# Value weights times the sums of four batches, a store for each head, loops written out

## The reference

```python
qh = (q_in @ wq + bq).reshape(b, q_len, H, K)          # b 8, q_len 112, H 16, K 128
kh = concat((kv_in @ wk + bk).reshape(b, t, H, K), bias_k)   # t 375, +1
vh = concat((kv_in @ wv + bv).reshape(b, t, H, K), bias_v)
weights = softmax(einsum('bqhk,bthk->bhqt', qh, kh) / sqrt(K))
ctx = einsum('bhqt,bthk->bqhk', weights, vh)
x = x + ctx @ wo + bo
```

## Time and profile before

| | us |
|---|---|
| median of 3 timed runs | 2390.0 (2389.4 to 2391.0) |
| the profiled execution | 2393.2 |
| its span, first to last instruction | 2391.3 |
| PE busy in it | 2313.3 (97%) |
| DVE busy | 1342.9 (56%) |
| ACT busy | 1146.4 (48%) |
| POOL busy | 376.4 (16%) |
| granted TensorE clock, mean | 0.995 of full |

### The profile page before, as it was taken

How to read it: one execution, slowest core, us unless ns; L and a number is a source line. 1 busy time by engine, 2 the same in 40 slices (tenths; PEclk the granted TensorE clock), 3 DMA queues, 4 the chain that set the end, 5 groups by cost and what they waited for, 6 DMA issues and landing times.

```text
span 2391.3 us, 45273 instructions
## 1 busy us (share of the span) xinstructions
PE 2313.3 (97%) x13859; PEld 2103.7 (88%) x13859; DVE 1342.9 (56%) x3154; ACT 1146.4 (48%) x2531; POOL 376.4 (16%) x739
## 2 busy tenths in 40 slices
PE   6899899999999999999999999999999999999999
PEld 5677678888999998999998788999998999998888
DVE  5677774443556555565554514555565555554743
ACT  4677752354445544445453444454444455453421
POOL 4011126430000100100101120001001001002421
PEclk9999989999999999999999999999999999999999
DMA  5322126474455645645635464455545546544110
GB/s 167 123 77 84 61 80 220 176 238 138 162 184 184 192 172 183 206 170 181 225 129 169 174 180 130 167 186 188 202 163 179 206 162 211 193 137 153 58 54 31
DMA packets 232451, 376.32 MB, mean 157 GB/s; under 512 B 57278, under 2 KB 185682, under 8 KB 232258
## 3 DMA queue, kind: packets, MB, share of 16 engines
q1 hardware_dynamic: 232258, 373.87, 47.0%
HBM read 315.77 MB, written 58.05 MB: 156 GB/s over the span
## 4 chain that ended last, share of the span: by engine, by line
PE 90%; DVE 3%; issue 3%; ACT 3%; DMA 0%; ACTq 0%; SPq 0%; DVEq 0%
PE ps_k L1508 10%; PE ps_k L1509 9%; PE ps_k L1510 9%; PE ps_o L1508 9%; PE ps_o L1510 8%; PE ps_o L1509 8%; PE ps_v L1508 6%; PE ps_v L1509 6%; PE ps_v L1510 6%; PE ps_s L1508 4%; PE ps_s L1510 4%; PE ps_s L1509 4%; PE ps_t L1667 3%; PE ps_t L1607 1%; PE ps_o L1619 1%
## 5 line engine op out<-in xcount | busy, mean ns | idle before, releaser
L1508 PE MATMUL ps_k<-cs_hi,w_a_hi 128*128 128x376 f32 x1152 | 391.7, 340 | 7.0 <-DVE k_lo L1284 4.3
L1509 PE MATMUL ps_k<-cs_lo,w_a_hi 128*128 128x376 f32 x1152 | 385.4, 335 | 0.0
L1510 PE MATMUL ps_k<-cs_hi,w_a_lo 128*128 128x376 f32 x1152 | 384.2, 333 | 0.0
L986 ACT ACTIVATE prob<-ps_s,row_columns 112x376 f32<-112x376 f32 x256 | 147.2, 575 | 300.3 <-DVE row_columns L1290 300.3
L767 POOL CAST k_hi<-xk_hi 128x1 fp32r x256 | 47.0, 184 | 1274.4 <-PE ps_s L1510 1274.4
L1508 PEld LDWEIGHTS ps_k<-cs_hi,w_a_hi 128*128 128x128 f32 x1152 | 217.3, 189 | 12.6 <-DVE k_lo L1284 8.8
L1509 PEld LDWEIGHTS ps_k<-cs_lo,w_a_hi 128*128 128x128 f32 x1152 | 217.5, 189 | 0.1
L1510 PEld LDWEIGHTS ps_k<-cs_hi,w_a_lo 128*128 128x128 f32 x1152 | 217.0, 188 | 0.0
L1284 DVE SCALAR_TENSOR_TENSOR k_lo<-ps_k,col_b,k_hi 128x375 fp32r<-128x375 f32 x256 | 155.2, 606 | 99.3 <-ACT k_hi L954 94.7
L954 ACT ACTIVATE k_hi<-ps_k,col_b 128x375 fp32r<-128x375 f32 x256 | 146.3, 572 | 102.2 <-PE ps_k L1510 99.3
L731 POOL TENSOR_TENSOR w_b_lo<-w_raw_b,w_b_hi 128x512 fp32r<-128x512 f32 x88 | 120.0, 1391 | 420.4 <-ACT w_b_hi L817 420.3
(11 more groups left out here) (256 smaller groups left out, 5964.0 us busy)
## 6 DMA issues: line engine op xcount, KB each, us to landing
ckd_hi<-context_by_key_halves SPq DMA_DIRECT2D x64, 768.0 KB, 4.3
ckd_lo<-context_by_key_halves SPq DMA_DIRECT2D x64, 768.0 KB, 5.8
cs_hi<-context_halves SPq DMA_DIRECT2D x64, 752.0 KB, 5.9
cs_lo<-context_halves SPq DMA_DIRECT2D x64, 752.0 KB, 7.3
w_raw_b<-in_blocks_b SPq DMA_DIRECT2D x104, 256.0 KB, 3.9
w_raw_a<-in_blocks_a SPq DMA_DIRECT2D x104, 256.0 KB, 4.6
q<-q_scratch SPq DMA_DIRECT2D x72, 224.0 KB, 5.7
shared<-extra_probability SPq DMA_DIRECT2D x32, 448.0 KB, 4.6
```

Of the source, the lines that this page charges most:

```text
L986: act.activation(prob[buf][0:LQ, 0:KW], ps_s[buf][0:LQ, 0:KW], ACT.Exp, bias=max_neg[0:LQ, buf:buf + 1], accum_out=prob_sum[0:LQ, buf:buf ...
L1508: pe.matmul(out, w_h, m_h, start=first, stop=False)
L1509: pe.matmul(out, w_h, m_l, start=False, stop=False)
L1510: return pe.matmul(out, w_l, m_h, start=False, stop=last)
```

## The change

- **Four batches at once.** Sums are kept for four batches (`sums`, a quad) and a head's product has 448 columns: 12 matmuls a head and quad. The heads of a quad come in steps 0 and 1 of the second batch of the next quad (`quarter == 1`), two a step; all other batches have one sum a step. Between heads there is one bank as before.
- **One `term` buffer** instead of two, with 448 columns. ACT's term of head t waits for DVE's add of head t-1.
- **One store a head**: four stores of 224 KB for each quad in 448-byte pieces, from two buffers `o_head`; `output` of head t waits for the store of head t-2. The SP queue stores heads 0 and 1 right after `load_halves`, heads 2 and 3 after `store_extra`.
- **The extra probabilities** are loaded once a quad, for four batches.
- **All five loops are written out** (`range` in place of `Fori`).
- **First attention**: the scores of tile t+2 are made before the weighted sums of tile t, and two tiles' scores stand in the prologue.
- **The MLP's end**: rows 0 and 1 are scaled before the weight splits, not after.
- Buffers of stages that don't overlap share memory.

```diff
+        self.quads = blocks * QUADS + pair // 2
+        self.quarter = self.b % 4
...
+        sums_hi = sb("sums_hi", [P, DT, 4 * HALF], F32R)
...
+        sums_lo = sb("sums_lo", [P, DT, 4 * HALF], F32R)
...
+        extra_b = extra[:, 0:4 * NT * LQ].rearrange("p (b r t) -> p b t r", b=4, t=NT)
+        term = extra[:, 4 * NT * LQ:5 * NT * LQ].rearrange("p (b r) -> p b r", b=4)
...
+        o_head = [o_all[:, HALF * i:HALF * (i + 1)].rearrange("p (b r) -> p b r", b=4) for i in range(2)]
...
-            with eng.Fori(1, 3) as fg:
+            for fg in range(1, 3):
                 mlp(0, fg, 1, RT * (fg + 1))
             mlp(0, 3, 1, RT * 4, norm=2)
...
-            with eng.Fori(0, 2) as a:
+            for a in range(0, 2):
...
-            with eng.Fori(1, PAIRS - 1) as p:
+            for p in range(1, PAIRS - 1):
...
-            with eng.Fori(1, GROUPS - 1) as group:
+            for group in range(1, GROUPS - 1):
...
-            if place.parity == 0:
+            if place.quarter != 1 or place.head:
                 return (t,)
             return {2: (0, 1), 3: (2, 3)}.get(t, ())
...
-            return (2 * t, 2 * t + 1) if place.parity and not place.head and t < 2 else ()
-
-        def second_late(place, t):
...
+            return (2 * t, 2 * t + 1) if place.quarter == 1 and not place.head and t < 2 else ()
+
+        def quad_before(place):
...
-                def store_pair(place):
-                    sp.wait_ge(z_ev, NT * place.pairs + NT)
+                def store_head(place, t):
+                    sp.wait_ge(z_ev, NT * place.quads + t + 1)
                     sp.sem_inc(sp_waited, 1)
-                    dst = o_scr[ds(place.group, 1), ds(2 * place.pair, 2)].rearrange("g b p f -> p (g b) f")
-                    sp.dma_start(dst, o_all[:, 0:2 * NT * LQ].rearrange("p (b f) -> p b f", b=2)).then_inc(z_out, 16)
+                    b0 = place.b - place.quarter
+                    dst = o_scr[place.group, b0:b0 + 4, :, t * LQ:(t + 1) * LQ].rearrange("b p r -> p b r")
+                    sp.dma_start(dst, o_head[t % 2]).then_inc(z_out[t % 2], 16)
...
-                    if not place.head:
-                        sp.wait_ge(z_term, NT * place.pairs)
-                        sp.sem_inc(sp_waited, 1)
-                    src = pex_scr[ds(place.block, 1), ds(2 * place.pair, 2)].rearrange("o b f -> o (b f)")
-                    sp.dma_start(shared[:, 0:2 * NT * LQ], src.partition_broadcast(P)).then_inc(extra_in, 16)
+                    wait(sp, z_term, NT * place.quads)
+                    sp.sem_inc(sp_waited, 1)
+                    src = pex_scr[ds(place.block, 1), ds(place.b - 3, 4)].rearrange("o b f -> o (b f)")
+                    sp.dma_start(extra[:, 0:4 * NT * LQ], src.partition_broadcast(P)).then_inc(extra_in, 16)
...
+                    for head in heads(place, 0):
+                        store_head(quad_before(place), head)
                     store_extra(place)
-                    if place.parity:
-                        if not place.head:
-                            store_pair(pair_before(place))
+                    for head in heads(place, 1):
+                        store_head(quad_before(place), head)
+                    if place.quarter == 3:
                         load_extra(place)
...
-                    if t >= 2 or not place.head:
-                        act.wait_ge(z_ev, NT * place.pairs + t - 1)
+                        act.wait_ge(extra_in, 16 * place.quads + 16)
+                    wait(act, z_ev, NT * place.quads + t)
                     act.sem_inc(act_waited, 1)
-                    act.activation(term[t % 2], extra_b[:, :, t, :], ACT.Identity,
+                    act.activation(term, extra_b[:, :, t, :], ACT.Identity,
...
-                for r in range(3 if norm is not None else 0):
-                    deviation(norm, r)
+                if norm is not None:
+                    for r in range(3):
+                        deviation(norm, r)
+                    scaled(norm, 0)
+                    scaled(norm, 1)
+                    deviation(norm, 3)
                 split_hi(0, na + 1, range(4), lambda s: (h_mm, HIDDEN * (4 * m + fg) + HIDDEN - 4 + s + 1))
                 if norm is None:
                     split_hi(1, nb + 1, range(4), lambda s: (y_mm, x0 + RT))
-                for r in (3, 4) if norm is not None else ():
-                    deviation(norm, r)
-                    for row in TURNS_LATE[r]:
+                if norm is not None:
+                    deviation(norm, 4)
+                    for row in (2, 3, 4):
                         scaled(norm, row)
-                if norm is not None:
-                    scaled(norm, 3)
-                    scaled(norm, 4)
                     deviation(norm, 5)
                     deviation(norm, 6)
...
-                    dve.wait_ge(z_mm, NT * place.pairs + t + 1)
-                    dve.wait_ge(z_term, NT * place.pairs + t + 1)
-                    if t == 0 and not place.head:
-                        dve.wait_ge(z_out, 16 * place.pairs)
-                    if t == 0 and place.head:
+                    dve.wait_ge(z_mm, NT * place.quads + t + 1)
+                    dve.wait_ge(z_term, NT * place.quads + t + 1)
+                    wait(dve, z_out[t % 2], 16 * (2 * place.quads + t // 2))
+                    if t < 2 and place.block == GROUPS * a and place.quads == QUADS * place.block:
                         for i in (2, 3):
                             dve.wait_ge(q_out[i], 16 * stores_before(i, 1, a + 1, 0))
-                    dve.tensor_tensor(o_pair[:, :, t, :], final_bank(place, t)[:, 0:2 * LQ].rearrange("p (b r) -> p b r", b=2),
-                                      term[t % 2], ALU.add).then_inc(z_ev, 1)
+                    dve.tensor_tensor(o_head[t % 2], final_bank(place, t)[:, 0:HALF].rearrange("p (b r) -> p b r", b=4),
+                                      term, ALU.add).then_inc(z_ev, 1)
...
+                    score_quad(place, 1)
 
                 def one_batch(place):
                     for t in range(NT):
-                        if place.key(t + 1):
-                            score_quad(*place.key(t + 1))
                         for j in range(SUB0):
                             turn(place, t, j)
                             kind, part = fill(place, t, j)
@@ -1642,6 +1655,8 @@
                                 key(*part)
                             if kind == VALUE:
                                 value(*part)
+                        if place.key(t + 2):
+                            score_quad(*place.key(t + 2))
                         weighted(place, t)
...
-                    if place.final and t > 1:
-                        pe.wait_ge(z_ev, NT * place.pairs + t - 1)
-                    elif not place.final and (t or not place.head):
-                        pe.wait_ge(z_ev, NT * place.pairs + t)
+                    wait(pe, z_ev, NT * place.quads + (t - 1 if place.final and t else t))
                     for c in range(DT):
                         if t == 0:
                             pe.wait_ge(c_lo, NT * place.visit + c + 1)
-                        last = product(final_bank(place, t)[:, 0:2 * LQ], [w[1][s][:, c, t * P:(t + 1) * P] for s in range(2)],
-                                       [heads_view(act_t[s][:, c, :], t) for s in range(2)], c == 0, c == DT - 1)
+                        last = product(final_bank(place, t)[:, 0:HALF], [w[1][s][:, c, t * P:(t + 1) * P] for s in range(2)],
+                                       [heads_view(sums[s][:, c, :], t) for s in range(2)], c == 0, c == DT - 1)
```

86 lines of the change are left out of this document (44 added, 42 removed).

## The result

The changed kernel is slower: 2415.4 us as a median (six runs, 2406.0 to 2421.8) against 2390.3 (2389.4 to 2396.3). The ratio is 1.0101 (95% interval 1.0089 to 1.0113). The forecast was 2369.2, with a range up to 2385: it had the wrong sign. The profiled execution took 2416.0 us with a span of 2414.2; before it took 2393.2, 22.8 us less.

A forecast was written before the change was run, and what follows sets the result against it. The prediction took PE, busy 97% of the span, as the bound. Its terms, -13.8 - 9.7 + 3.5 + 17 - 16.3 + 3 - 3 - 1.5 = -20.8 us, took 2390.0 to 2369.2 us; range 2347 to 2385.

The forecast's parts named there:

- head products, waits before heads: Second attention: merged 448-column products -13.8 us, no wait before the second head -9.7, third head waiting for DVE's add +3.5.
- store of head 0: Second attention: the store lands behind the context loads, delaying head 2's add and PE's head 3: 1.2 us a quad, +17.
- loops: Jumps of the group and layer loops: PE's gaps and the slow clock behind them go, -16.3 us (12 to 20 less).
- ends of the attentions: Last batch of each second attention: two short waits more for softmax in each of two layers, +3 us (0 to +5).
- first attention's order: First attention, scores ahead of weighted sums: nothing won in the middle, last batch gains, -3 us (8 less to 2 more).
- first MLP's end: First MLP's end: scalings ahead of weight splits remove PE's 1.27 us wait for ACT, -1.5 us with what follows.
- the bound of 32 us: Upper bound of the head 0 store stall: if the load takes 8.1 us, 2.3 us a quad, +32.
- The other three stores of a quad go out on a quiet queue: Second attention, SP queue: only the store of head 0 queues behind loads; no cost was counted for the others.
- (a): Rival: the store doesn't hold up head 3, so the 17 us go: 2352.2 us, 2348 with larger loop gain; chance 0.26.
- (b): Rival: stores in 448-byte pieces are slow while loads stream beside them, 48 us in place of 17: 2400 us; chance 0.06.
- (c): Rival: the long straight program makes PE pause for instructions elsewhere, the 16.3 us come back: 2385.5 us; chance 0.06.
- my main case: The forecast itself, with a store stall of 0.5 to 2.3 us a quad: 2359 to 2385 us; chance 0.58.

The follow-up runs named there:

- combined: Changed kernel with the store of head 0 ahead of the loads, the first attention and first MLP's end in old order, outputs' split behind the last sums: 2346.3 us.
- experiment 1: Changed kernel with the store of head 0 issued ahead of the two halves of the next context instead of behind them: 2371.3 us, ratio 0.9907.
- experiment 5: The kernel before with only its five loops written out (`range` in place of `Fori`): 2375.0 us, ratio 0.9931.
- experiment 7: Changed kernel with ACT's and DVE's split of the first landed outputs moved behind the last sums of each second attention: 2405.2 us, ratio 1.0062.
- experiment 6: Changed kernel with the first attention in the old order: 2409.6 us; in reverse, the combined kernel with the new order put back: 2357.2 us.
- experiment 8: Changed kernel with the store of head 0 ahead of the context's halves, plus the first MLP's end in the old order: 2370.0 us, ratio 0.9913.
- experiment 2: Changed kernel with each store of a head written in 1792-byte pieces instead of 448, same place in the queue: 2415.5 us, ratio 1.0099.
- experiment 3: Changed kernel with the store of head 0 issued from ACT's own queue instead of SP's, at the same time: 2420.4 us, ratio 1.0113.

## Why the prediction was wrong, step by step

| term | predicted | measured | from |
|---|---|---|---|
| head products, waits before heads (-13.8 - 9.7 + 3.5) | -20.0 | -30.6 | second attentions, combined against loops written out only: -15.7, -14.9 |
| store of head 0 | +17 | +45 | experiment 1 |
| loops | -16.3 | -16.8 | experiment 5 |
| ends of the attentions | +3 | +10.2 | experiment 7 |
| first attention's order | -3 | +10.9 | experiment 6, in the combined kernel |
| first MLP's end | -1.5 | +2.0 | experiment 8, by the stages of the traces |
| sum | -20.8 | +20.7 | the result: +25.0 by medians, +22.8 by the profiled runs |

- **The store** is the term of the sum that decided, and the mechanism was the one described. A quad that starts at 684.70 would reach head 3 after 12.5 us without the wait, as forecast; the second half was issued at 5.1 (forecast 5.2), the store at 5.7 (6.0). The step that failed is the landing: 14.6 us instead of 12.6, because I took the 7.2 us of one load, less 0.4 for an older backlog, where the ones in front of these stores took 7.3 to 8.8 (8.1 as a mean). At a threshold every microsecond of error counts in full: 1.2 us a quad became 2.2. The 8.1 us of the earlier trace rows would have given it; it was used as the bound only, and the bound of 32 us met the waits (31.1). What stood in no term is their tail, 14 us, mostly at the slow level, although had shown one. With +45 for +17 the sum alone would have been 2397, so this term by itself turned the sign. "The other three stores of a quad go out on a quiet queue" was wrong too, for the store of head 1 (issued at 692.56, it took 7.7 us), but nothing waited for it.
- **Rivals.** (a) fell (experiment 1: it does hold up head 3), (b) fell (experiment 2), (c) fell (experiment 5). What came true was my main case with a larger price, which I had not let reach past 2385; that the time lies even past (b)'s 2400 says nothing for (b).
- **First attention.** The step looked at was judged rightly: from the scores at 191.15 to the next turn at 192.58 are 1.43 us, as many as from 191.62 to 193.05 before. What failed is "in the middle nothing is won" as a bound of zero for the other three steps: the scores' wait for the last maximum, in one step covered by the time that PE waited anyway, appears in a step that had no wait (198.84), and turns wait for ACT more often (0.82 us at 187.48). That zero is 10 to 11 us, the whole of the term. In the last batch the waits, forecast 2 us shorter, grew by 1, as scores wait 2.5 to 2.7 us for the maxima there.
- **Ends.** I counted two short waits more in a layer. They are there (1.0 and 0.7 us), but one of 1.2 us stood there before, so they add 0.4. What I missed is that ACT's own program has a wait for a landing between the sums, and that these sums now come sooner after the last scores, while the landing doesn't (experiment 7).
- **MLP's end.** The wait of 1.27 us is gone, as forecast. I wrote that the splits, 2.9 us later, are needed only from 493 us on. That they are later by about this much is right (3.2 us); what I left out is what runs beside them: POOL's half of the split moved onto DVE's casts, and the next wait, 0.64 us at 496.52 before, is 2.71 us.
- **Loops**: right, -16.3 against -16.8 by medians. By the two profiled runs it is -21, of which 17.5 lie in the three stages where I counted.
- **Head products**: right in kind, too small by 10.6 us. The waits were sized well (distances that begin with a key product, the one before a second head among them, fell from 0.1747 to 0.1717 us, 4.6 us a layer; forecast 4.85). The heads' own products cost 0.1149 us per 224 columns as a mean over all (loops written out only), against 0.111 in the middle of a head, as each head begins and ends with a slower distance and there are now half as many heads; and the third head waits 0.16 us (692.28 to 692.62 against 0.17), not 0.25. The context sums too got closer, 0.2023 us from one to the next as a mean instead of 0.2051. That is some 5 us, of which 2 come back at the turns behind them; I can't explain it.

## What to carry to other kernels

When a wait is at a threshold, size it with the slowest of the rows that stand where the new one will stand, and add the slow clock behind it. Issue what someone waits for ahead of the bulk loads: the same store cost 45 us behind two of them and nothing ahead of them. And for each moved instruction ask also what now runs beside it, on the engines that hinder each other and in the programs of the engines that wait in order.

## What the runs showed of the hardware

- A second queue is no second path: 224 KB issued from ACT's queue landed 9.4 us later, with two loads of 752 KB in flight from SP's (experiment 3; 8.7 to 9.8 us in 13 quads of 14).
- DVE's cast of 128x512 took 0.40 us alone and 1.42 to 1.51 us while POOL ran its subtractions, the subtraction beside it 0.69 and 1.66 (experiment 8). The Trainium skill (SBUF — State Buffer, Who interferes with whom) says that the two share a port pair, which the one that issues first holds for its whole instruction while the other is blocked, when DVE's instruction is a cast in a mode that uses both ports or has two inputs in SBUF. The trace agrees: POOL's four instructions took 1.3 to 1.7 us each, and a cast's delay of 1.0 us fits into one. Which mode the cast ran in, no run shows.
- After a wait of 2.9 us at 700 us PE's clock was at the 1.2 GHz level for 3.4 us (from 701.6), in the middle of a stage that had been at 2.4 GHz throughout. The length of the wait alone didn't decide: of the 14 waits, those of 2.87, 2.45, 2.15, 2.88, 2.15 and 2.64 us were followed by such a stretch, and the other eight, up to 2.75 us, were not.
